# Two-layer attention on one core: side products moved to single banks, one query stack, a three-pair ring, and three kinds of step on GpSimd

## The reference, cut to what matters

```python
# layer 0, 8 heads of 32
xn  = (x - mean_c(x)) / sqrt(var_c(x) + eps) * gamma
q, k, v = split(w_qkv @ xn)
sim = (q^T k) * 32**-0.5 + bias(head)          # 1024 x 1024 per head; bias from a small MLP
x1  = w_out @ (v softmax(sim)^T) + x
# layer 1, one head
f, g, h = Wf x1 + bf, Wg x1 + bg, Wh x1 + bh   # f, g: 32 rows, h: 256 rows
out = gamma * (h softmax(f^T g)) + x1
```

## Time and profile before

| what | value |
|---|---|
| time, three runs | 1782.32, 1785.84, 1788.01 us; median 1785.84 |
| the profiled execution's own time | 1790.26 us |
| its span in the trace | 1788.5 us |
| busy share PE / DVE / ACT / POOL | 89% / 83% / 77% / 0% |
| set-up, until the first score tile reaches DVE | 98.5 us |
| element 0; element 4 (as 1 to 6); element 7; tail | 187.7; 205.6; 197.5; 68.0 us |
| element 4 by phase: rows 0, columns 0, rows 1, columns 1 | 55.0, 48.1, 60.2, 42.3 us |

### The profile page before, as it was taken

One profiled execution on the slowest core, in us unless ns is written; L12 is line 12 of the kernel. 1 busy time (PEld: TensorE's weight loads), 2 busy tenths in 40 slices (PEclk: granted clock), 3 DMA queues, 4 the chain that ended last, 5 costly groups with the idle time before them and its releaser, 6 DMA issues.

```text
span 1788.5 us, 18614 instructions
## 1 busy us (share of the span) xinstructions
PE 1589.6 (89%) x5976; PEld 753.9 (42%) x5976; DVE 1477.8 (83%) x2168; ACT 1382.2 (77%) x2033; POOL 7.1 (0%) x5
## 2 busy tenths in 40 slices
PE   6078899899998999889998999989998999999988
PEld 2043335345353544435453443535444453535424
DVE  3067988898988989898888989899889989899853
ACT  2067889788888878878787888878798887889743
POOL 1000000000000000000000000000000000000000
PEclk9577869999999999999999999999999999999999
DMA  5941204320350203501151203502043203400100
GB/s 129 248 138 36 59 1 132 93 59 1 100 148 1 60 1 107 142 25 35 48 165 37 59 1 107 142 1 60 25 124 101 60 1 90 136 1 0 39 10 23
DMA packets 57257, 122.71 MB, mean 69 GB/s; under 512 B 21428, under 2 KB 22964, under 8 KB 57160
## 3 DMA queue, kind: packets, MB, share of 16 engines
q1 hardware_dynamic: 54344, 115.37, 23.5%
q10 hardware_dynamic: 2816, 6.16, 1.3%
HBM read 78.92 MB, written 44.13 MB: 69 GB/s over the span
## 4 chain that ended last, share of the span: by engine, by line
PE 51%; DVE 24%; issue 18%; DMA 3%; ACT 3%; DVEq 0%; ACTq 0%; SPq 0%
DVE biased L1005 13%; PE psum L527 9%; PE psum L602 9%; PE psum L629 8%; PE psum L581 6%; PE psum L407 6%; DVE biased L1019 5%; PE psum L582 4%; PE psum L450 4%; DMA q_stack<-q_parts 2%; PE psum L460 2%; PE psum L484 1%; ACT probs L836 1%; DVE probs L931 1%; DVE x L954 1%
## 5 line engine op out<-in xcount | busy, mean ns | idle before, releaser
L1005 DVE CUSTOM_DVE_ANT_0 biased<-psum,bias_lines_sb 128x1024 f32<-128x1024 f32 x512 | 617.1, 1222 | 174.1 <-PE psum L582 163.0
L819 ACT ACTIVATE biased<-biased,nmax 128x1024 f32<-128x1024 f32 x512 | 587.4, 1148 | 162.5 <-DVE nmax L1005 157.9
L836 ACT ACTIVATE probs<-biased 128x1024 f32<-128x1024 f32 x512 | 536.8, 1057 | 128.6 <-DVE biased L1019 107.5
L1019 DVE TENSOR_TENSOR biased<-psum,bias_lines_sb 128x1024 f32<-128x1024 f32 x512 | 597.8, 1216 | 45.7 <-PE psum L602 33.4
L602 PE MATMUL psum<-q_stack,k_stack 98*128 98x512 f32 x1024 | 392.8, 490 | 38.5 <-DVE nmax L1005 15.9
L581 PE MATMUL psum<-k_stack,q_stack 96*128 96x512 f32 x512 | 331.1, 647 | 102.5 <-DMA q_stack<-q_parts 46.8
L602 PEld LDWEIGHTS psum<-q_stack,k_stack 98*128 98x128 f32 x1024 | 178.9, 200 | 328.8 <-issue 150.8
L629 PE MATMUL psum<-probs,vT 128*32 128x512 f32 x2048 | 285.1, 627 | 6.2 <-DVE st L886 3.9
L581 PEld LDWEIGHTS psum<-k_stack,q_stack 96*128 96x128 f32 x512 | 100.0, 195 | 287.1 <-DVE nmax L1005 165.8
L582 PE MATMUL psum<-k_stack,q_stack 96*128 96x512 f32 x512 | 210.8, 412 | 0.0
L527 PE MATMUL psum<-probs 128*128 128x512 f32 x384 | 186.6, 592 | 0.0
(11 more groups left out here) (78 smaller groups left out, 1090.9 us busy)
## 6 DMA issues: line engine op xcount, KB each, us to landing
q_stack<-q_parts SPq DMA_DIRECT2D x90, 256.0 KB, 5.3
k_stack<-k_parts SPq DMA_DIRECT2D x45, 512.0 KB, 7.3
q_parts<-st SPq DMA_DIRECT2D x15, 1024.0 KB, 3.9
k_parts<-st SPq DMA_DIRECT2D x15, 1024.0 KB, 4.3
xn<-in_x_dram SPq DMA_DIRECT2D x8, 1024.0 KB, 8.9
x<-in_x_dram SPq DMA_DIRECT2D x8, 1024.0 KB, 9.6
out_dram<-x SPq DMA_DIRECT2D x8, 1024.0 KB, 4.1
bias_lines_sb<-bias_lines SPq DMA_DIRECT2D x32, 240.0 KB, 15.1
```

The lines of the kernel that those rows point to most:

```text
L819: nc.scalar.activation(biased[:, m % BIASED, :], biased[:, m % BIASED, :], ACT.Exp, scale=-1.0, bias=nmax[:, m:m + 1], accum_out=rowsum[:, ...
L836: nc.scalar.activation(probs[:, n % P_SLOTS], biased[:, n % BIASED, :] .rearrange("p (i n) -> p i n", i=2), ACT.Exp).then_inc(SEMS["probs_ ...
L1005: nc.vector.tensor_tensor_reduce(biased[:, m % BIASED, :], pair(bank_of(g, first, ("rows", m))), bias_lines[:, g * HG + h, a0:a0 + N], -1. ...
L1019: nc.vector.tensor_tensor(biased[:, n % BIASED, :].rearrange("p (i n) -> p i n", i=2), psum[:, bank:bank + 2, :], bias_lines[:, g * HG + 2 ...
```

## The change

Five things are done at once.

1. **Staging and stacks.** `st` becomes `st_k` and `st_q`. `q_stack` has one place instead of two; it is refilled by halves: the half for queries 0 to 511 when the column tiles of the first half are done, the other when all are. k of group 1 (`k1`) is no longer made in rows 0 of its own element but in columns 1 of the one before, q of group 1 (`q1`) stays in rows 0. In the set-up k1 of element 0 is made as well.
2. **Single banks.** Every side product is 128 x 512 at most, in bank 4 or 5 (the last of h in 6). A table written by `in_sides` lists the users of each bank in order, and `side_bank` makes PE wait for the evacuation of the one before. mean, variance, f, q, k come in halves; v and h come as two 256-column products in one bank, taken out by one copy.
3. **Ring.** In rows 0 the ring has three pairs (0, 2, 6); in rows 1 two, as before.
4. **GpSimd.** It adds the two channel halves before the mean and before the variance (so PE needs one matmul for each half of the columns, not two), multiplies by `rstd`, and adds `bh` to h, which ACT has copied out of PSUM. `hT` has its own tile.
5. **Set-up.** SP loads the bias lines of heads 0 and 1 and makes the lines of group 1, then waits for q and k of element 0 to have arrived before it loads the other six heads.

```diff
-        st = sb("st", [P, 2, N], F32R)
-        q_stack = sb("q_stack", [KS + 2, G, NHALF, HG, HALF], F32R)
+        st_k = sb("st_k", [P, 2, N], F32R)
+        st_q = sb("st_q", [P, 2, N], F32R)
+        q_stack = sb("q_stack", [KS + 2, NHALF, HG, HALF], F32R)
...
-        side_0 = [(3 + i, "q", i) for i in range(QUANTA)] + [(6, "high_q", 0), (8, "low_q", 0)]
-        side_0 += [(4 + t, "v", t) for t in range(NT)] + [(3 + t, "keep_v", t) for t in range(NT)]
-        side_0 += [(11 + i, "k", i) for i in range(QUANTA)] + [(14, "high_k", 0), (16, "low_k", 0)]
+        side_0 = [(3 + t, "v", t) for t in range(NT)] + [(4 + 2 * i, "keep_v", i) for i in range(NT // 2)]
+        side_0 += [(11 + a, "q1", a) for a in range(QUANTA)]
+        side_0 += [(12 + 2 * half, "high_q1", half) for half in range(NHALF)]
+        side_0 += [(13 + 2 * half, "low_q1", half) for half in range(NHALF)]
...
-        side_0 += [(20 + i, "mean", i) for i in range(QUANTA)] + [(23, "centre", 0), (24, "square", 0)]
-        side_0 += [(24 + i, "f", i) for i in range(QUANTA)] + [(27, "high_f", 0), (29, "low_f", 0)]
-        side_0 += [(27 + i, "var", i) for i in range(QUANTA)] + [(30, "rstd", 0)]
-        side_1 = [(3 + t, "h", t) for t in range(NT)] + [(3 + t, "keep_h", t) for t in range(NT)]
+        side_0 += [(22, "sum_x", 0)]
+        side_0 += [(24 + a, "f", a) for a in range(QUANTA)]
...
+        side_0 += [(28 + half, "mean", half) for half in range(NHALF)] + [(30 + half, "centre", half) for half in range(NHALF)]
+        side_0 += [(30 + t, "h", t) for t in range(2)]
+        column_0 = [(0, "keep_h", 0), (0, "square", 0), (1, "square", 1), (1, "sum_squares", 0)]
+        column_0 += [(2, "g", 0), (3, "g", 1), (4, "high_g", 0), (5, "low_g", 0)]
+        column_0 += [(7, "var", 0), (8, "ln_var", 0), (10, "var", 1), (11, "ln_var", 1), (11, "rstd", 0)]
+        column_0 += [(12, "norm", 0), (12, "norm", 1)]
+        column_0 += [(13, "g", 2), (14, "g", 3), (15, "high_g", 1), (16, "low_g", 1)]
+        column_0 += [(22, "h", 2), (23, "h", 3), (24, "keep_h", 1), (26, "h", 4), (27, "h", 5), (28, "keep_h", 2)]
+        column_0 += [(30, "k0", 0), (31, "k0", 1)]
+        side_1 = [(0, "high_k0", 0), (1, "low_k0", 0), (3, "h", 6), (4, "h", 7), (5, "keep_h", 3)]
         for t in range(NT):
-            at = 6 + 8 * t // 3
+            at = 3 + 3 * t
             side_1 += [(at, "s1", t), (at, "max1", t), (at, "exp1", t), (at + 2, "invert", t), (at + 2, "scale_h", t)]
             side_1 += [(at + 4 + i, "sa", QUANTA * t + i) for i in range(QUANTA)]
+        for kind, half, one, two in (("k0", 1, 2, 3), ("q0", 0, 7, 8), ("q0", 1, 13, 14), ("k1", 0, 23, 24),
+                                     ("k1", 1, 28, 29)):
+            column_1 += [(one, kind, 2 * half), (two, kind, 2 * half + 1), (two + 1, "high_" + kind, half),
+                         (two + 2, "low_" + kind, half)]
...
-        column_0 = [(1, "rstd", 1), (3, "norm", 0), (9, "norm", 1)]
-        for kind, half, one, two in (("g", 0, 2, 4), ("g", 1, 8, 10), ("k0", 0, 14, 16), ("k0", 1, 24, 26)):
-            column_0 += [(one, kind, 2 * half), (two, kind, 2 * half + 1), (two + 1, "high_" + kind, half),
-                         (two + 3, "low_" + kind, half)]
-        for kind, half, one, two in (("q0", 0, 4, 6), ("q0", 1, 12, 14)):
...
-            banks = [(0, 2)[(n - columns) % 2] for n in range(columns)]
+            slots = S_SLOTS if g == 0 else 2
+            banks = [(0, 2, 6)[(n - columns) % slots] for n in range(columns)]
...
+            def side_bank(kind, arg, b):
+                before = SIDE_BEFORE[kind, arg, b]
+                if before is not None:
+                    was, i, e = before
+                    if was in QK:
+                        need(pe, "lo_ready", e, split(was, i))
...
+                    elif was == "var":
+                        need(pe, "rstd_ready", e, i + 1)
+                    elif was == "h":
+                        need(pe, "h_kept", e, i + 1)
+                    elif was == "pv":
+                        need(pe, "o_ready", e, i + 1)
...
+            lines_out(0)
+            bias_in(0)
+            bias_in(1)
+            lines_out(1)
+            for half in range(NHALF):
+                need(sp, f"q_loaded_{half}", 0, Q_DMAS)
+            need(sp, "k_loaded", 0, K_DMAS)
+            bias_in(2)
+            bias_in(3)
+            k_out(sp, 0, 1)
+            k_in(sp, 0, 1)
+            for h in range(HG, G * HG):
+                bias_in(h)
...
+                if kind == "sum_x":
+                    nc.gpsimd.tensor_tensor(x_sum, xn[:, 0, :], xn[:, 1, :], ALU.add).then_inc(SEMS["x_summed"], 1)
+                elif kind == "sum_squares":
+                    nc.gpsimd.tensor_tensor(square_sum, squares[:, 0, :], squares[:, 1, :],
+                                            ALU.add).then_inc(SEMS["squares_summed"], 1)
+                elif kind == "norm":
+                    nc.gpsimd.tensor_tensor(xn[:, arg, :], xn[:, arg, :], rstd, ALU.mult).then_inc(SEMS["normed"], 1)
+                elif kind == "keep_h":
+                    nc.gpsimd.tensor_tensor(hT[:, 2 * arg:2 * arg + 2, :], hT[:, 2 * arg:2 * arg + 2, :], bh_all[:],
+                                            ALU.add).then_inc(SEMS["h_ready"], 1)
```

544 lines of the change are left out of this document (301 added, 243 removed).

## The result

The changed kernel takes **1914.01 us** (median of 4 runs, 1909.22 to 1919.63) against 1786.71 for the kernel before: ratio 1.0718, 95% interval 1.0681 to 1.0756. I had forecast 1778 with a range of 1730 to 1815. The profiled execution took 1916.59 us, its span 1914.7.

What follows compares the result with a forecast made beforehand. Bound: three nearly balanced in-order engines plus hand-off losses, none full. Span 1788.5 + 33 (six steady elements) - 5 (element 0) - 5 (element 7) - 27 (set-up) - 4 (tail) = 1780.5; forecast 1778 us, range 1730 to 1815.

Steps and rivals of the forecast that it cites:

- Columns 0 and 1: Column phases of a steady element: PE and DVE waits would lengthen columns 0 by 4.5 us and columns 1 by 8.3.
- Rows 0: First row phase of a steady element: bunched products gone and a deeper ring, 53.0 us, so -2.0.
- Rows 1: Second row phase of a steady element: one s1 in three slots instead of 2.67, 55.6 us, so -4.6.
- Element 0: First element: loses the wait for x and the q and k pairs in rows 0, gains k1; -5 us.
- cover: Set-up: SP issues the second eight loads from about 71 us; head 2 is needed by tile 8, some 14 us later.
- Set-up: Before the first tile: 8.9 MB to move at 230 GB/s, first tile near 70, -27 us, bounds -37 and -20.
- GpSimd: GpSimd's adds and multiplications: 5.2 or 7.3 us an element by rows, 13.5 by the skill, inside the slack; no cost.
- third rival: GpSimd holds DVE's tiles up, 7.3 us an element, 1829 us in all; chance 0.07.
- Tail and element 7: End of the run: tail -4 us as g waits less and h is done before s1; element 7 -5 us.
- Rival 2: Column phases: more waits and a lower PE clock, +11 us a steady element, 1811 us in all; chance 0.20.

Runs made afterwards that it cites:

- e11: Kernel before, with the second half of k0 in columns 0 at slots 22 and 23 instead of 24 and 26; 1808.7 us, ratio 1.013.
- e13: e9 with DVE's shift chain of columns 0 at slot 2 instead of slot 4; 1759.9 us.
- e6: Changed kernel with pv ahead of the side products of its pair of slots on PE, in both column phases; 1833.3 us.
- e2: Changed kernel with the first two parts of h moved from slots 30 and 31 of rows 0 to slots 0 and 1 of columns 0; 1896.9 us.
- e9: Changed kernel with pv first, first h parts in columns 0, one h pair moved to rows 1, and five columns 1 products later; 1774.1 us.
- e15: e9 with s1 in rows 1 placed as in the kernel before: first at slot 6, then 2.67 slots apart, instead of 3 and three; 1801.0 us.
- e17: e13 with the loads of heads 4 to 7 moved on SyncE behind the first store of shift rows of element 0; 1744.5 us.
- e14: e9 with every GpSimd step of the phases narrowed to 8 columns, leaving out most of its work; 1755.7 us.
- e3: Changed kernel with four parts of h in columns 0 moved from slots 22, 23, 26, 27 to 24, 25, 27, 28, copies also later; 1917.3 us.
- e4: Changed kernel with the five products of columns 1 moved to later slots, k1 from 23, 24 and 28, 29 to 25 and 29; 1879.2 us.

## Why the prediction was wrong, step by step

**Columns 0 and 1 (said +4.5 and +8.3, measured +11.2 and +11.6).** This is the step that failed. The stops of PE stood where I had said, behind slot 22 and at k1; the step from the stop to its price was wrong. I followed each chain from DVE or ACT to the product that needs a bank, and on to "the next tile's matmuls". I did not ask what else is queued on PE behind the waiting product. It was pv, whose end ACT's exponential needs, whose end the next copy needs: a loop, not a chain. Of this the trace before had 2.1 us of L836, a size that I read as none, and e11 shows that one pair of products moved closer turns it into 24.1. In element 3 DVE was idle 17.3 and 12.1 us in the two phases, where I had 13.8 and 7.7.

The rest of the miss in columns 0 is DVE's busy time, 42.0 where I had 38.8. Some 2 us of that are the step held beside GpSimd, a cost that I had put at nothing (e13). So it is partly luck that columns 0 of e6, 50.9, comes so near my 52.6: it still holds this cost, and its products stand later than those that I summed. PE's largest single stop in columns 0 was the wait for low_g, 4.06 us in element 3; I had named this wait and given it no size of its own.

**Rows 0 (said -2.0, measured +1.5).** The place was named ("needs the centre step of slot 30, which costs DVE 1.9"), its size was off. PE stopped 2.63 us there, and before that 2.15 us for low_f, a stop that I had not named; the products behind the two took 2.07 and 2.03, at 1.2 GHz. With h moved (e2, e9) the phase is 52.8 and 51.6, under my 53.0.

**Rows 1 (said -4.6, measured 0.1).** The terms of my sum can be read in element 3: slots 0 to 6 11.8 (said 11.7), the last seven slots 10.7 (said 10.7), but the six periods 37.6 where I had 33. The first one holds the wait for the scaled h and the first products at 1.2 GHz, and takes 7.4:

```profile
858.33 2.04 PE L614 MATMUL psum<-probs,hT 128*128 128x512 f32 x2 [0.68 <-ACT hT L856]
...
861.37 1.22 DVE L1111 CUSTOM_DVE_ANT_0 biased<-psum,bias_lines_sb 128x1024 f32<-128x1024 f32 x1 [2.22 <-PE psum L665]
```

A plain period is 5.67; the three with the logarithm, the shift chain and the turn take 6.1, 6.1 and 6.7, which I had counted at nothing. My own terms (11.7, 33 and 10.7) sum to 55.4, not 55.6. That the three-slot spacing helps was right (e15).

**Element 0 (said -5, measured +13).** I named as cover that head 2 comes in time. It nearly did (DVE waits 1.7 us for a load of bias lines). What I did not follow is x, queued on the same SyncE behind the sixteen last loads: 15.7 us. e17 takes it back.

**Set-up (said -27, bounds -37 and -20; measured -33.2).** Within its bounds, near the one of the larger gain: from 31 to 65 the DMA engines moved 244 GB/s, 8.3 MB, where I had taken 8.9 MB at 230.

**GpSimd (said nothing; measured some 2 us an element).** The prices were low: an add of 1024 columns takes 2.37 us where DVE's row gave 1.215. The figure of the Trainium skill (GPSIMD Engine Reference, 3.1 Elementwise, 4497 ns for 2048) gives an estimate of 2.25, and of 13.5 us an element. The trace is near both, with 2.37 and 14.7. None of these steps came late, as I said, but for element 0's sum of x, whose x came late. The third rival in its wide form is excluded, tiles stay at 1.22. Its narrow form, "only the short shift chains are held, some 2 us an element at most", which I had by the rule of the Trainium skill and then dropped with the rival, is what e13 and e14 measured.

**Tail and element 7 (said -9, measured 0).** Not followed up.

**The rivals.** Rival 2 had the direction and both parts, stops behind one-slot chains and the lower clock, but priced them at +11 for a steady element, where +24.5 was measured. Its price was twice the forecast's +5.5; no rival had a wait that brings the next one. The range ended at 1815 for the same reason.

## What to carry to other kernels

Where a product is moved towards the step that it waits for, list everything that stands behind it in its queue, and follow who waits for each of these. If the list leads back to the engine that it waits for, the stop brings the next one, and its price is more than the wait: 1.6 times it in e11, the only run that adds such a stop alone. Let the work that others wait for go first, and put optional work behind it; a queue's set-up loads are to be ordered by first use, all of them, including those of the next stage.

PE runs up to three tiles ahead here. A product one or two slots behind the output copy that it needs stopped PE for 2.0 to 2.6 us; three slots behind it there was no stop (k0, kernel before) or 0.30 us (h, e3). Behind the copy of h the stops were 0.75 and 0.9 us at two slots (changed kernel) and 2.42 and 1.31 at one (e3). So the distance alone does not give the price.

## What the runs showed of the hardware

- A DVE step of 0.17 us took 2.18 us (two inputs in SBUF) or 2.27 us (a copy of 128x16 with one input) when it began beside a GpSimd add of 2.36 or 2.37 us, and ended with the add; a DVE tile with one operand in PSUM kept 1.22.
- GpSimd: add or multiplication of 128x1024 f32 2.34 to 2.42 us, about twice DVE's 1.215; add of 128x512 1.26 to 1.30 us.
- PE behind a stop of 2.05 to 2.63 us: the products of a bank (two of 512 columns or four of 256) took 1.91 to 2.07 us in place of 1.02 to 1.13, and the granted clock of columns 1 of element 3 was 0.88 in the changed kernel and 0.97 in e4. Behind five of the seven stops of about 2 us in e11, and the seven of 0.97 us at slot 22 in e6, it did not fall.
